# A two-layer graph kernel on one core: the last six adjacency blocks summed by column group, and what follows them reordered

## The chip, the cores and the metric

The kernel runs on one core of a Trainium2 chip. The metric is the device time of one execution in microseconds (us), smaller is better; times are medians of several runs. TensorE is called PE in the profile, VectorE DVE, ScalarE ACT, GpSimd POOL, SyncE SP. "PEld" is TensorE's weight load.

## The reference, cut to what matters

`x` is 4096 x 128, `adj` is 4096 x 4096, everything f32.

```python
def _gcn_norm_dense(adj):
    A = adj + jnp.eye(n)
    deg = A.sum(axis=1)
    d = jnp.where(deg > 0, jax.lax.rsqrt(deg), 0.0)
    return d[:, None] * A * d[None, :]
def _L0(x, adj, W1, b1, W2, b2):
    An = _gcn_norm_dense(adj)
    h = jax.nn.relu(An @ (x @ W1) + b1)
    return An @ (h @ W2) + b2                      # the second aggregation
def _L1(x, adj, ff0_w, ff1_w, attn_w, g1, b1, g2, b2):
    x_norm = _ln(x, g1, b1)
    mask = (adj > 0) | jnp.eye(n, dtype=bool)
    for i in range(K):                             # K = 2 heads
        h = x_norm @ ff0_w[i].T
        s_src, s_dst = h @ attn_w[i, :c], h @ attn_w[i, c:]
        e = leaky_relu(s_src[:, None] + s_dst[None, :])
        atten = softmax(where(mask, e, NEG), axis=1)
        att = _ln(atten @ h + x, g2, b2)
        h_next = h_next + jax.nn.elu(att @ ff1_w[i].T) / K
    return h_next
x = _layernorm(x + _L0(...)); x = _layernorm(x + _L1(x, adj, ...))
```

## The kernel before, in words

**Stages.** The 4096 nodes are 32 blocks of 128 rows, or 8 column groups of 512. The first aggregation reads all of `adj` and of its transpose and takes the degrees from them. The second reads the transpose again: each of 32 turns (a block of 128 x 4096, 2 MB) adds 8 matmuls of 128x512, one into each of PSUM's eight banks, so that bank k holds the sum of column group k. Each turn also makes the block's 0/1 mask in bytes and stores it in DRAM (`mask`, 0.5 MB). Then comes attention, whose passes of 4 phases x 16 chunks read the masks back: ScalarE makes `T` (two relus for a chunk), VectorE multiplies it by the mask, TensorE sums 4 matmuls of 128x512.

**What sets the order.** Every engine's program is written out by hand, with semaphores; an engine runs its list strictly in order, and a DMA is issued by the engine that stands in its place in the list (loads by SP, mask stores by ScalarE).

**The second aggregation.** Turns 0 to 3 use blocks still in `colbuf` (four slots), turns 4 and 5 the two slots of `rowbuf` (`AHEAD = 2`), turns 6 to 31 `colbuf` again. `reload` in the SP program (L321) loads the next block into a slot once TensorE (`pe_block`) and the mask of the slot's turn (`mask_made`) are done with it. VectorE adds the identity to the block's own columns (`add_self`, L747), on which TensorE waits (`own_ready`), and makes the mask (`make_mask`, L751 and L754) in one of two `mtile` slots, once the store of two turns ago has landed. ScalarE copies the turn's weights to `stat` and issues the store (`supply`, L497 and L499); its copy for a turn begins when TensorE has finished the turn before the last.

```python
AHEAD = LATE = 2
ROUNDS = NI - 2                 # NI = 8, four turns in a round
```

**The end of it.** The last `LATE = 2` turns go by column group (L1189): for group k, two matmuls, then for group k-1 the turn of the sum (`L1200`, four transposes), for group k-5 the turn of the normalised nodes (`L1206`), for group k-6 the source and target terms (`wag`, four matmuls of 128x4 into bank 0). Between them stand ScalarE's copies out of PSUM (L515, L519), VectorE's skip, statistics and normalisation (L795, L778, L785, L807) and GpSimd's inverse roots (L418 to L426, one group after the other). GpSimd's (POOL's) two powers for a group are `rstd` and `r2`.

**From there to the first chunk.** VectorE makes `st` from all terms (L815, L818) and its largest values over the free axis (`span`). TensorE turns `st`, ScalarE copies it to `s_rows` and stores it in DRAM (`s_src`), SP loads it back as `Rrow`, spread over all partitions (L337). GpSimd's `partition_all_reduce` (L428) gives the maximum over nodes, `top`. TensorE multiplies eight pairs of node blocks by `gff` into PSUM banks 4 to 7 (`multiply_z`, 0 to 7, 2 matmuls of 128x256 each), ScalarE copies them to `W` (`read_z`, L530); the other eight pairs follow one by one behind chunks 0 to 7, their copies behind relus 5 to 12. ScalarE then copies `mixed`, loads its table of exponentials, makes `ratio` and `weight` (L544, L545), the exponential of `Rrow` (L550) and the first relus (L558).

Of the kernel before, what the change touches and what calls it, by code (L numbers as in the profile page):

```python
# [16 lines left out]
F32 = mybir.dt.float32  # L17
# [3 lines left out]
ALU = mybir.AluOpType  # L21
# [3 lines left out]
P = 128  # L25
# [39 lines left out]
def build(nc, t, out):  # L65
# [16 lines left out]
    with ctx:  # L82
# [29 lines left out]
        half = sb("half", [P, B], F32)  # L112
        d_all = sb("d_all", [P, B], F32)
# [8 lines left out]
        span = sb("span", [P, 2 * K], F32)  # L122
        top = sb("top", [P, 2 * K], F32)
# [54 lines left out]
        Rrow = sb("Rrow", [P, 2, WIDE], F32)  # L178
# [8 lines left out]
        def sems(names):  # L187
# [19 lines left out]
            "x1_ready x1t_done x1T_ready st_done st_step st_ready s_turned s_copied s_stored")  # L207
        mix_turned, mixT_ready, mix_done, mix_ready, z_done, z_read = sems(
            "mix_turned mixT_ready mix_done mix_ready z_done z_read")
        span_step, span_ready, top_ready, npass_step, npass_ready = sems("span_step span_ready top_ready npass_step npass_ready")  # L210
# [49 lines left out]
        AHEAD = LATE = 2  # L260
        ROUNDS = NI - 2
# [4 lines left out]
        STATS, MOMENTS, SHIFT = 1, 2, 3  # L266
        TURN = SHIFT + 1
        ZR = B // 2
        Z_EARLY = 8
        PHASE = NC  # L270

        def more_passes(eng):

            eng.wait_ge(npass_ready, 1)
            return eng.value_load(npass[0:1, 0:1], min_val=0, max_val=MAX_PASSES)

# [21 lines left out]
        def _(sp):  # L298
# [45 lines left out]
            def phase(q, g, next_h, f):  # L344
                for c in range(NC):
# [4 lines left out]
                    if c == 6:  # L350
                        if not (isinstance(q, int) and g == 0):
                            sp.wait_ge(relu_made, at_turn(q * (G * NC) + g * NC))
                        source_row(next_h, (g + 1) % G)
                    if c == NC - 1 and f is not None:
                        store(f, (g - 2) % G)

            sp.wait_ge(agg_done, 2 * NG)
# [3 lines left out]
            sp.wait_ge(s_stored, 16)  # L361
            source_row(0, 0)
# [16 lines left out]
        def _(pool):  # L379
# [6 lines left out]
            pool.tensor_copy(ident_u8[:, :], ident[:, :]).then_inc(ident_ready, 1)  # L386
            pool.memset(keeps[:, 0:1], 1.0).then_inc(consts_ready, 1)
# [28 lines left out]
            for k in range(NG):  # L416
# [4 lines left out]
                pool.wait_ge(scale_ready, k + 1)  # L421
                r = r2[:, group(k)]
                pstep(pool.tensor_tensor(r, rstd[:, group(k)], rstd[:, group(k)], ALU.mult))
                pstep(pool.tensor_tensor(r, r, mv[:, group(k), 1], ALU.mult))  # L424
                pstep(pool.tensor_scalar(r, r, LN_EPS, 1.0, ALU.add, ALU.mult))  # L425
                pool.tensor_tensor(r, r, half[:, group(k)], ALU.pow).then_inc(r2_ready, 1)  # L426
            pool.wait_ge(span_ready, 1)
            pool.partition_all_reduce(top[:, :], span[:, :], P, bass.bass_isa.ReduceOp.max).then_inc(top_ready, 1)  # L428
# [34 lines left out]
        def _(act):  # L463
# [42 lines left out]
            for u in range(LATE):  # L506
                supply(B - LATE + u, u, ROUNDS * RING + AHEAD + u, u % SN)

            for i in range(NG + TURN + 2):
                k = i  # L510
                if k < NG:
                    act.wait_ge(agg_done, NG + k + 1)
                    if k >= SN:
                        act.wait_ge(tr_done, k - 1)
                    act.activation(hT[:, k % SN, :], ps[:, k, :], ACT.Copy).then_inc(accT_ready, 1)  # L515
                k = i - TURN - 1
                if 0 <= k < NG:
                    act.wait_ge(x1t_done, k + 1)
                    act.activation(x1T[:, cols(k, GW)], ps[:, k, :], ACT.Copy).then_inc(x1T_ready, 1)  # L519

            act.wait_ge(s_turned, 1)
            act.activation(s_rows[:, :], ps[0:K * B, 1, 0:P], ACT.Copy).then_inc(s_copied, 1)
            act.wait_ge(s_copied, 1)
            act.dma_start(s_dram.rearrange("k (b p) -> (k b) p", p=P), s_rows[:, :]).then_inc(s_stored, 16)
            act.wait_ge(mix_turned, 1)
            act.activation(mixT[:, :, :].rearrange("p k c -> p (k c)"), ps[:, 2, 0:K * C], ACT.Copy).then_inc(mixT_ready, 1)

            def read_z(r):
                act.wait_ge(z_done, r + 1)
                act.activation(W[:, Z0:Z1 + 1:2, 2 * r:2 * r + 2, :],  # L530
                               ps[:, 4 + r % 4, :].rearrange("p (b h c) -> p h b c", b=2, h=K), ACT.Copy).then_inc(z_read, 1)

            for r in range(Z_EARLY):
                read_z(r)
            act.wait_ge(mix_done, 1)
            for head in range(K):
                at = head * C
                act.activation(mixed[:, head, at:at + C], ps[:, 3, cols(head)], ACT.Copy).then_inc(mix_ready, 1)
# [115 lines left out]
        def _(v):  # L654
# [114 lines left out]
            for u in range(LATE):  # L769
                v.wait_ge(col_loaded[u], 16 * (NI + 1 + ROUNDS))  # L770
                add_self(colbuf[:, u, :], ROUNDS * RING + AHEAD + u)
                v.wait_ge(own_ready, ROUNDS * RING + AHEAD + u + 1)
                make_mask(B - LATE + u, colbuf[:, u, :], ROUNDS * RING + AHEAD + u, u % SN, 16 * ((B - LATE + u) // SN + 1))
# [16 lines left out]
            for i in range(NG + 3):  # L790
                k = i
                if k < NG:
                    v.wait_ge(tr_done, k + 1)
                    for b in range(k * BPG, (k + 1) * BPG):
                        last = v.scalar_tensor_tensor(out=x1[:, b, :], in0=ps[:, k, cols(b % BPG)],  # L795
                                                      scalar=d_all[:, b:b + 1], in1=x1[:, b, :],
                                                      op0=ALU.mult, op1=ALU.add)
                    last.then_inc(rows_ready, 1)
                if 0 <= i - STATS < NG:
                    stats(i - STATS)  # L800
                if 0 <= i - MOMENTS < NG:
                    moments(i - MOMENTS)
                if 0 <= i - SHIFT < NG:
                    k = i - SHIFT
                    v.wait_ge(scale_ready, k + 1)
                    for b in range(k * BPG, (k + 1) * BPG):
                        last = v.tensor_scalar(x1[:, b, :], x1[:, b, :], mv[:, b, 0:1], rstd[:, b:b + 1],  # L807
                                               ALU.subtract, ALU.mult)
                    last.then_inc(x1_ready, 1)


            v.wait_ge(st_done, NG)
            v.wait_ge(r2_ready, NG)
            v.wait_ge(consts_ready, 5)
# [198 lines left out]
            v.wait_ge(top_ready, 1)  # L1013
            v.tensor_copy(gref[:, CUR:CUR + 1], top[:, 0:1]).then_inc(gref_step, 1)
            v.tensor_copy(gref[:, TOP1:TOP1 + 1], top[:, 1:2])
            v.wait_ge(gref_step, 1)
            set_window(0, 0)
            set_inside(0, 0, 0)
            set_inside(0, 0, 1)
            cap_row(0, 0)  # L1020
# [296 lines left out]
```

## Time and profile before

| | us |
|---|---|
| median of 3 runs (lowest, highest) | 1063.94 (1062.9, 1065.08) |
| the profiled execution, its own time | 1063.9 |
| its span, first to last instruction | 1062.1 |
| TensorE busy in the span | 986.0 (93%) |
| VectorE, ScalarE, GpSimd busy | 701.0, 499.0, 113.6 |
| mean granted clock of TensorE | 0.967 of full |

Times in the rows count from the span's start. The second aggregation runs from 288.4 to some 500 us, the first chunk begins at 554.59 us. In a timeline row, "x8" merges eight records in a row, the number in square brackets is the engine's idle time before the first and what ended it. One f32 matmul of the program leaves two records, each transpose one. In a row of windows, "PEclk" is the granted clock as a share of full speed.

### The profile page before, as it was taken

What the parts mean: (1) busy time and instruction counts of PE and PEld (TensorE: products, weight loads), DVE (VectorE), ACT (ScalarE), POOL (GpSimd) and SP (SyncE); (2) the same over time, 40 slices, a digit from 0 to 9 for tenths busy, and PEclk for the clock granted to TensorE, in tenths of its full rate; (3) what the DMA queues carried; (4) which work ended last, traced back from release to release, by engine and by line L of the source; (5) the groups of instructions that cost most, each with busy time, mean ns of one, the idle gap of its engine ahead of it and who ended that gap; (6) DMA issues with size and microseconds to landing.
All of it is one profiled execution on the core that took longest, in us unless ns stands there. A gap on an engine that the chain in (4) does not pass through costs nothing.

```text
span 1062.1 us, 9255 instructions
## 1 busy us (share of the span) xinstructions
PE 986.0 (93%) x2590; PEld 477.6 (45%) x2592; DVE 701.0 (66%) x1251; ACT 499.0 (47%) x723; POOL 113.6 (11%) x144
## 2 busy tenths in 40 slices
PE   5789999999999999999769999999999999999980
PEld 4334444444644444444655444444545444444440
DVE  0567766654355444344737767888799998988874
ACT  3433332221200000001266765978686888888754
POOL 0011111111040000000800000000010101010111
PEclk8899999999999999999769999999999999999995
DMA  9999999999286999995023131222222232323201
GB/s 347 427 426 427 428 426 425 425 422 388 110 322 256 371 377 383 385 380 213 1 70 99 62 97 59 91 79 97 72 70 86 84 99 89 99 90 100 84 5 40
DMA packets 62202, 226.03 MB, mean 213 GB/s; under 512 B 4496, under 2 KB 44112, under 8 KB 52048
## 3 DMA queue, kind: packets, MB, share of 16 engines
q1 hardware_dynamic: 57040, 208.56, 51.3%
q10 hardware_dynamic: 5120, 17.01, 4.0%
q8 instruction: 15, 0.25, 0.1%
q14 instruction: 27, 0.22, 0.1%
HBM read 205.59 MB, written 19.96 MB: 212 GB/s over the span
## 4 chain that ended last, share of the span: by engine, by line
PE 77%; DMA 11%; ACT 5%; POOL 3%; issue 2%; DVE 2%; SPq 1%; POOLq 0%; ACTq 0%; DVEq 0%
PE ps L1096 77%; DMA W<-in_adj 11%; ACT W L478 2%; POOL rstd L419 1%; POOL r L426 1%; ACT T L558 1%; ACT final L604 1%; SPq L302 0%; DVE T L870 0%; ACT mix L587 0%; ACT squares L578 0%; POOL rs L437 0%; POOL r L424 0%; POOL r L425 0%; POOLq L82 0%
## 5 line engine op out<-in xcount | busy, mean ns | idle before, releaser
L1096 PE MATMUL ps<-colbuf,stat 128*128 128x512 f32 x992 | 441.9, 602 | 25.3 <-DVE diag L712 24.8
L1096 PE MATMUL ps<-T,Yw 128*128 128x512 f32 x1024 | 445.1, 594 | 9.2 <-DVE T L870 9.2
L870 DVE SCALAR_TENSOR_TENSOR T<-T,mring 128x2048 f32<-128x2048 f32 x128 | 292.5, 2287 | 66.6 <-ACT T L558 65.9
L558 ACT ACTIVATE T<-Rrow,small,ratio 128x1024 f32<-128x1024 f32 x256 | 301.3, 1230 | 70.7 <-PE ps L1096 70.4
L1096 PEld LDWEIGHTS ps<-T,Yw 128*128 128x128 f32 x1024 | 195.4, 191 | 245.4 <-issue 230.7
L1096 PEld LDWEIGHTS ps<-colbuf,stat 128*128 128x128 f32 x992 | 187.9, 193 | 248.9 <-issue 220.8
L478 ACT ACTIVATE W<-W 128x4096 f32<-128x4096 f32 (+30 forms) x32 | 66.1, 2067 | 147.7 <-DMA W<-in_adj 147.7
L497 ACT ACTIVATE stat<-xw_g 128x128 f32 (+1 forms) x32 | 9.9, 310 | 197.8 <-PE ps L1096 167.8
L751 DVE TENSOR_SCALAR mtile<-colbuf 128x4096 uint8<-128x4096 f32 x30 | 69.7, 2323 | 11.6 <-DMA mask<-mtile 9.7
L747 DVE TENSOR_TENSOR colbuf<-colbuf,ident 128x128 f32 (+1 forms) x26 | 7.6, 291 | 88.3 <-DMA colbuf<-in_adjT 88.3
L672 DVE TENSOR_TENSOR W<-W,colbuf 128x3712 f32<-128x3712 f32 (+28 forms) x29 | 62.3, 2148 | 0.0
L394 POOL PARTITION_ALL_REDUCE colrow<-W x30 | 32.2, 1073 | 217.1 <-DVE W L672 186.3
L434 POOL TENSOR_SCALAR rs<-sumsq 128x4 f32<-128x4 f32 x16 | 14.3, 892 | 346.6 <-ACT squares L578 225.9
L683 DVE TENSOR_SCALAR small<-rowpart,colpart 128x1 f32<-128x1 f32 x30 | 6.4, 214 | 60.5 <-ACT W L478 60.4
L1096 PE MATMUL ps<-mixed,numS 128*128 (+1 forms) x128 | 30.6, 382 | 3.1 <-DVE A L933 1.9
L1096 PEld LDWEIGHTS ps<-mixed,numS 128*128 128x128 f32 x128 | 24.2, 190 | 13.6 <-issue 8.5
L945 DVE SCALAR_TENSOR_TENSOR mix<-A,inv,W 128x256 f32<-128x256 f32 x64 | 26.7, 480 | 3.3 <-DVE inv L940 3.1
L587 ACT ACTIVATE mix<-mix,rs 128x128 f32<-128x128 f32 (+1 forms) x64 | 20.4, 390 | 14.9 <-POOL rs L437 14.5
L604 ACT ACTIVATE final<-W,fin_shift,fin_scale 128x128 f32 (+1 forms) x48 | 19.5, 480 | 16.3 <-DVE fin_shift L992 16.0
L418 POOL TENSOR_SCALAR rstd<-mv 128x4 f32<-128x4 f32 x8 | 1.5, 194 | 196.7 <-DVE mv L785 196.1
L710 DVE TENSOR_TENSOR colbuf<-colbuf,ident 128x128 f32<-128x128 f32 x32 | 9.3, 292 | 16.7 <-DMA colbuf<-in_adjT 15.9
L860 DVE TENSOR_SCALAR Yw<-W,r2w,weight 128x128 f32<-128x128 f32 x64 | 19.0, 338 | 0.2
(150 smaller groups left out, 581.5 us busy)
## 6 DMA issues: line engine op xcount, KB each, us to landing
colbuf<-in_adjT SPq DMA_DIRECT2D x58, 2048.0 KB, 13.2
mring<-mask SPq DMA_DIRECT2D x128, 256.0 KB, 2.7
mask<-mtile ACTq DMA_DIRECT2D x32, 512.0 KB, 10.2
Rrow<-s_src SPq DMA_DIRECT2D x9, 512.0 KB, 4.1
W<-in_adj SPq DMA_DIRECT2D x2, 2048.0 KB, 14.7
W<-in_adjT SPq DMA_DIRECT2D x2, 2048.0 KB, 12.7
out<-final SPq DMA_DIRECT2D x6, 512.0 KB, 3.9
W<-in_xT SPq DMA_DIRECT2D x8, 256.0 KB, 6.9
```

Source lines behind the costliest of these rows:

```text
L394: pool.partition_all_reduce(colrow[:, b % 2, :], colacc[:, cols(b)], P, bass.bass_isa.ReduceOp.add)\
L434: pool.tensor_scalar(rs[:, half_of(part)], sumsq[:, half_of(part)], 1.0 / C, LN_EPS, ALU.mult, ALU.add)\
L478: act.activation(row, row, ACT.Copy, accum_out=rowpart[:, b % 2:b % 2 + 1]).then_inc(rowsum_done, 1)
L558: last = act.activation(T[:, c % TS, j, :], Rrow[:, g % 2, :], ACT.Relu, scale=ratio[:, c * JB + j:c * JB + j + 1], bias=small[:, 8:9])
L587: last = act.activation(mix[:, i, bass.ds(1 - h, 1), :].rearrange("p o c -> p (o c)"), mix[:, i, bass.ds(h, 1), :].rearrange("p o c -> p ( ...
L604: last = act.activation(final[:, i, :], W[:, bass.ds(dst, 1), k * GB + i, :].rearrange("p o c -> p (o c)"), ACT.Identity, scale=fin_scale[ ...
L672: v.tensor_tensor(colacc[:, lo:], colacc[:, lo:], colbuf[:, u, lo:], ALU.add).then_inc(colacc_done, 1)
L751: v.tensor_scalar(mtile[:, tile, :], block, 0.0, None, ALU.is_gt).then_inc(tile_step, 1)
L860: last = v.tensor_scalar(Yw[:, b, :], x1[:, b, :], r2w[:, b:b + 1], weight[:, b:b + 1], ALU.mult, ALU.add)
L870: v.scalar_tensor_tensor(out=tile, in0=tile, scalar=1.0, in1=mring[:, c % TS, :, :].rearrange("p b n -> p (b n)"), op0=ALU.add, op1=ALU.mu ...
L945: last = v.scalar_tensor_tensor(out=mix[:, i, :, :], in0=A[:, b, 0:2 * C].rearrange("p (o c) -> p o c", o=2), scalar=inv[:, i:i + 1], in1= ...
L1096: return pe.matmul(*args, skip_group_check=True, **kw)
```

## The change

Names are those of the changed kernel.

- `ROUNDS` is one less and `LATE` is 6: turns 26 to 31 are done by column group. Two of their blocks (26, 27) are loaded into `rowbuf` early, behind turns 4 and 5, the other four (22 to 25) into `colbuf` behind turns 22 to 25. Groups 0 and 1 take their first five matmuls each before either takes its sixth. The weights come straight from `xw_g`.
- VectorE adds the identity to all six blocks first, then makes the six masks.
- ScalarE issues the six stores, runs one small Exp (which loads its table), and only then copies sum 0.
- Skip, statistics and normalisation of a group follow each other on VectorE; the last two groups are interleaved; GpSimd puts off `r2` of the last two groups.
- Source terms of nodes 0 to 1023 are made, turned, stored and loaded ahead (`early_*`).
- The maximum over nodes: `span` turned by TensorE, a `tensor_reduce` on 4 partitions, and a matmul of `ones` by a diagonal of 4 columns.
- Z products 0 to 12 stand before chunk 0, between the turns of the last groups; three of them (10 to 12) are copied by VectorE; 13 to 15 follow chunks 0 to 2, their copies stand behind relus 1 to 3.

```diff
-        AHEAD = LATE = 2
-        ROUNDS = NI - 2
+        AHEAD = 2
+        LATE = AHEAD + RING
+        ROUNDS = NI - 3
-        Z_EARLY = 8
+        Z_FIRST, Z_MOVED, Z_BANKS = 10, 3, 4
+        Z_WAITING = Z_FIRST + Z_MOVED
+        EARLY = 6
 # SP, behind the first four reloads
+            for n in range(AHEAD):
+                sp.wait_ge(pe_block, RING + n + (1 + MASK_CREDIT))
+                sp.wait_ge(mask_made, RING + n + (1 + MASK_CREDIT))
+                sp.dma_start(late(n)[0], dram_block(adj_cols, late(n)[1])).then_inc(row_loaded[n], 16)
 # POOL
-            pool.partition_all_reduce(top[:, :], span[:, :], P, bass.bass_isa.ReduceOp.max).then_inc(top_ready, 1)
 # ACT
-            for u in range(LATE):
-                supply(B - LATE + u, u, ROUNDS * RING + AHEAD + u, u % SN)
+            for n in range(LATE):
+                turn = B - LATE + n
+                act.wait_ge(mask_made, turn + (1 + MASK_CREDIT))
+                act.dma_start(dram_block(mask_dram, late(n)[1]), mtile[:, turn % SN, :]).then_inc(mask_stored[turn % SN], 16)
+            act.wait_ge(zeros_ready, 2)
+            act.activation(small[:, 11:12], small[:, 8:9], ACT.Exp)
...
-                    if g == 0 and 5 <= c < 5 + ZR - Z_EARLY:
-                        read_z(Z_EARLY + c - 5)
+                    if g == 0 and 1 <= c <= ZR - Z_WAITING:
+                        read_z(Z_WAITING + c - 1)
 # DVE
+            for n in range(LATE):
+                block, b = late(n)
+                if n < AHEAD:
+                    v.wait_ge(row_loaded[n], NI * 32 + 32)
+                else:
+                    v.wait_ge(col_loaded[n - AHEAD], 16 * (NI + 1 + ROUNDS))
+                add_self(block, b)
+            for n in range(LATE):
+                turn = B - LATE + n
+                block, b = late(n)
+                v.wait_ge(own_ready, turn - RING + 1)
+                make_mask(turn, block, b, turn % SN, 16 * (turn // SN + 1))
...
+            v.wait_ge(span_turned, 1)
+            v.tensor_reduce(highest[:, :], ps[0:2 * K, 6, 0:P], AX_X, ALU.max).then_inc(top_step, 1)
...
+            for r in range(Z_FIRST, Z_FIRST + Z_MOVED):
+                v.wait_ge(z_done, r + 1)
+                v.tensor_copy(W[:, Z0:Z1 + 1:2, 2 * r:2 * r + 2, :],
+                              ps[:, 2 + r % Z_BANKS, :].rearrange("p (b h c) -> p h b c", b=2, h=K)).then_inc(z_moved, 1)
 # PE
+            for k in range(2):
+                late_sums(k, range(LATE - 1))
+            for k in range(2):
+                late_sums(k, [LATE - 1])
+            turn_sums(0)
+            for k in range(2, NG):
+                late_sums(k, range(LATE // 2))
+                turn_sums(k - 1)
+                late_sums(k, range(LATE // 2, LATE))
+                turn_nodes(k - 2)
+                if k == EARLY - 1:
+                    pe.wait_ge(early_ready, 1)
+                if k >= 3:
+                    sources(k - 3)
+                if k == EARLY:
+                    pe.transpose(ps[0:GB, 1, 0:P], early_st[:, :], ident[:, :]).then_inc(early_turned, 1)
+            turn_sums(NG - 1)
...
+            turn_nodes(NG - 2)
+            multiply_z(2)
+            sources(NG - 2)
+            for r in range(3, 7):
+                multiply_z(r)
+            turn_nodes(NG - 1)
+            multiply_z(7)
+            sources(NG - 1)
+            multiply_z(8)
...
-                    if g == 0 and c < ZR - Z_EARLY:
-                        multiply_z(Z_EARLY + c)
+                    if g == 0 and c < ZR - Z_WAITING:
+                        multiply_z(Z_WAITING + c)
```

ScalarE at the end of the second aggregation; `hT` is the copy of a group's sum, `W` here the copy of its turned nodes. Before:

```order
111 L497 ACTIVATE stat<-xw_g 128x128
112 L499 DMA mask<-mtile 128x4096
113 L497 ACTIVATE stat<-xw_g 128x128
114 L499 DMA mask<-mtile 128x4096
115 L515 ACTIVATE hT<-ps 128x512 x6
```

And in the changed kernel:

```order
111 L539 DMA mask<-mtile 128x4096 x6
112 L541 ACT_TABLE_LOAD
113 L541 ACTIVATE small<-small 128x1
114 L547 ACTIVATE hT<-ps 128x512 x3
115 L551 ACTIVATE W<-ps 128x512
```

Six stores and the table load, where two stores were, now stand ahead of the first copy of a sum.

VectorE in the same place of the changed kernel, with its waits; before, each addition of the identity (L747) was followed by its own block's mask (L751, L754):

```order
512 L793 TENSOR_TENSOR colbuf<-colbuf,ident 128x128 [waits col_loaded2]
513 L793 TENSOR_TENSOR colbuf<-colbuf,ident 128x128 [waits col_loaded3]
514 L797 TENSOR_SCALAR mtile<-W 128x4096 [waits mask_stored0,own_ready]
515 L800 TENSOR_TENSOR mtile<-mtile,ident_u 128x128 [waits tile_step]
516 L797 TENSOR_SCALAR mtile<-W 128x4096 [waits mask_stored1,own_ready]
517 L800 TENSOR_TENSOR mtile<-mtile,ident_u 128x128 [waits tile_step]
```

Even the masks of the two blocks that were loaded early (`W`) now stand behind the wait for the last block to arrive (`col_loaded3`).

ScalarE at the first chunks (`T` a relu, `W` the copy of a z product). Before:

```order
130 L558 ACTIVATE T<-Rrow,small,ratio 128x1024 x12
131 L530 ACTIVATE W<-ps 128x2x256
132 L558 ACTIVATE T<-Rrow,small,ratio 128x1024 x2
```

And in the changed kernel:

```order
140 L604 ACTIVATE T<-Rrow,small,ratio 128x1024 x4
141 L555 ACTIVATE W<-ps 128x2x256
142 L604 ACTIVATE T<-Rrow,small,ratio 128x1024 x2
143 L555 ACTIVATE W<-ps 128x2x256
```

The first copy of a z product stood behind the relus of six chunks; it now stands behind those of two.

## Rows read from the trace of the kernel before

**Rows 1.** The page's busy times, then the chain of waits, in order of time

```profile
PE 986.0 (93%) x2590; PEld 477.6 (45%) x2592; DVE 701.0 (66%) x1251; ACT 499.0 (47%) x723; POOL 113.6 (11%) x144
...
286.68 207.69 PE ps L1096 x487
...
554.59 94.61 PE ps L1096 x240
```

**Rows 2.** Timeline of ScalarE from 465 us: the copy that begins when turn 25 ends

```profile
467.02 0.31 ACT L497 ACTIVATE stat<-xw_g 128x128 f32 x1 [6.56 <-PE ps L1096]
```

**Rows 3.** VectorE's timeline: identity additions in turns 29 and 31, each ending a load's wait

```profile
477.92 0.29 DVE L747 TENSOR_TENSOR colbuf<-colbuf,ident 128x128 f32 x1 [3.53 <-DMA colbuf<-in_adjT]
...
491.14 0.29 DVE L747 TENSOR_TENSOR colbuf<-colbuf,ident 128x128 f32<-128x128 f32 x1 [3.98 <-DMA colbuf<-in_adjT]
```

**Rows 4.** Instructions on `colbuf`, 286 to 500 us: time of its loads

```profile
DMA to landing us min/median/max: 8.5/10.7/11.4
```

**Rows 5.** VectorE's timeline: the second and third mask, whose stores meet no loads

```profile
292.62 2.29 DVE L751 TENSOR_SCALAR mtile<-colbuf 128x4096 uint8<-128x4096 f32 x1
...
295.44 2.29 DVE L751 TENSOR_SCALAR mtile<-colbuf 128x4096 uint8<-128x4096 f32 x1 [0.21 <-DMA mask<-mtile]
```

**Rows 6.** Windows: span of time, PE, PEld, DVE, ACT, POOL busy, clock, DMA share, GB/s

```profile
326.00:330.00 4.00, 4.00 (x11) 1.85 (x10) 3.23 (x4) 0.00 (x0) 0.00 (x0) 1.00 0.05 18
...
516.00:520.00 4.00, 2.44 (x23) 2.21 (x22) 4.00 (x21) 1.10 (x2) 3.42 (x8) 1.00 0.00 0
...
524.00:536.00 12.00, 9.86 (x47) 9.61 (x47) 3.50 (x16) 1.79 (x3) 7.42 (x16) 0.50 0.01 1
...
548.00:552.00 4.00, 0.00 (x0) 0.00 (x0) 0.99 (x4) 3.86 (x6) 0.00 (x0) 0.87 0.00 0
```

**Rows 7.** Timeline of the last two turns, by group (PE), with ScalarE's copy

```profile
496.83 0.60 ACT L515 ACTIVATE hT<-ps 128x512 f32<-128x512 f32 x1 [2.14 <-PE ps L1096]
...
498.35 0.60 PE L1200 MATMUL ps<-ident,hT 128*128 128x128 f32 x4
...
498.79 1.88 PE L1096 MATMUL ps<-colbuf,stat 128*128 128x512 f32 x4
...
500.51 0.60 PE L1200 MATMUL ps<-ident,hT 128*128 128x128 f32 x4
...
512.28 0.95 PE L1096 MATMUL ps<-wag,W 128*128 128x4 f32 x8
```

**Rows 8.** Timeline from the last source terms to the maximum over nodes

```profile
536.21 0.29 DVE L815 TENSOR_TENSOR st<-ps,r 128x128 f32<-128x128 f32 x1 [4.42 <-PE ps L1096]
...
538.60 0.39 POOL L428 PARTITION_ALL_REDUCE top<-span  x1 [5.95 <-issue]
```

**Rows 9.** Timeline from the last z copy before the chunks to chunk 1

```profile
544.00 0.75 DVE L844 TENSOR_SCALAR Rrow<-Rrow,gref 128x1024 f32<-128x1024 f32 x1 [4.06 <-DMA Rrow<-s_src]
...
546.48 0.44 ACT L538 ACTIVATE mixed<-ps 128x128 f32<-128x128 f32 x2
546.94 1.28 ACT L544 ACT_TABLE_LOAD   x1
548.24 0.23 ACT L544 ACTIVATE ratio<-below 128x32 f32<-128x32 f32 x1
...
548.62 1.06 ACT L550 ACTIVATE Rrow<-Rrow 128x1024 f32<-128x1024 f32 x1
...
552.25 2.29 DVE L870 SCALAR_TENSOR_TENSOR T<-T,mring 128x2048 f32<-128x2048 f32 x1 [2.57 <-ACT T L558]
...
554.59 5.26 PE L1096 MATMUL ps<-T,Yw 128*128 128x512 f32 x8 [8.20 <-DVE T L870]
```

**Rows 10.** Timeline of TensorE, then of ScalarE, at the first chunks

```profile
559.69 1.03 PE L1096 MATMUL ps<-gff,W 128*128 128x256 f32 x4
560.55 3.60 PE L1096 MATMUL ps<-T,Yw 128*128 128x512 f32 x8
...
564.19 2.38 ACT L558 ACTIVATE T<-Rrow,small,ratio 128x1024 f32<-128x1024 f32 x2 [1.93 <-PE ps L1096]
```

More of the change, by code:

```diff
@@ L332, in _ @@
                     reload(u, i * RING + (AHEAD + u), i * RING + (AHEAD + u))
-            for u in range(LATE):
+            for u in range(RING):
                 reload(u, ROUNDS * RING + AHEAD + u, ROUNDS * RING + AHEAD + u)
@@ L350, in phase @@
                     if c == 6:
-                        if not (isinstance(q, int) and g == 0):
+                        if isinstance(q, int) and g == 0:
+                            sp.wait_ge(s_stored, 16)
+                        else:
                             sp.wait_ge(relu_made, at_turn(q * (G * NC) + g * NC))
@@ L414, in pstep, with scale_rows @@
                 pool.wait_ge(pool_step, done[0])
-            for k in range(NG):
+            def scale_rows(k):
                 pool.wait_ge(moments_ready, k + 1)
@@ L789, in _, with add_skip @@
             v.wait_ge(skip_ready, NG)
[L790 to L809, printed above, removed]
+            def add_skip(k):
+                v.wait_ge(tr_done, k + 1)
+                for b in range(k * BPG, (k + 1) * BPG):
+                    last = v.scalar_tensor_tensor(out=x1[:, b, :], in0=ps[:, k, cols(b % BPG)],
+                                                  scalar=d_all[:, b:b + 1], in1=x1[:, b, :],
+                                                  op0=ALU.mult, op1=ALU.add)
+                last.then_inc(rows_ready, 1)
+                stats(k)
+                moments(k)
@@ new lines, in late_sums @@
+            def late_sums(k, some):
+                for n in some:
+                    block, b = late(n)
+                    if k == 0:
+                        if n < AHEAD:
+                            pe.wait_ge(row_loaded[n], NI * 32 + 32)
+                        else:
+                            pe.wait_ge(col_loaded[n - AHEAD], 16 * (NI + 1 + ROUNDS))
+                        pe.wait_ge(own_ready, ROUNDS * RING + AHEAD + n + 1)
+                    last = multiply(ps[:, k, :], xw_g[:, b, :], block[:, cols(k, GW)], start=False, stop=n == LATE - 1)
+                if n == LATE - 1:
+                    last.then_inc(agg_done, 1)
@@ new lines, in turn_sums, with turn_nodes @@
+            def turn_sums(k):
+                pe.wait_ge(accT_ready, k + 1)
+                for ib in range(BPG):
+                    last = pe.transpose(ps[:, k, cols(ib)], hT[:, k % SN, cols(ib)], ident[:, :])
+                last.then_inc(tr_done, 1)
+            def turn_nodes(k):
+                pe.wait_ge(x1_ready, k + 1)
+                for ib in range(BPG):
+                    last = pe.transpose(ps[:, k, cols(ib)], x1[:, k * BPG + ib, :], ident[:, :])
+                last.then_inc(x1t_done, 1)
@@ new lines, in sources, with multiply_z @@
+            def sources(k):
+                pe.wait_ge(x1T_ready, k + 1)
+                for ib in range(BPG):
+                    b = k * BPG + ib
+                    last = multiply(ps[:, 0, cols(b, 2 * K)], x1T[:, cols(b)], wag[:, :], start=True, stop=True)
+                last.then_inc(st_done, 1)
+            def multiply_z(r):
+                if r >= Z_FIRST + Z_BANKS:
+                    pe.wait_ge(z_moved, r - Z_FIRST - Z_BANKS + 1)
+                elif r >= Z_BANKS:
+                    pe.wait_ge(z_read, r - Z_BANKS + 1)
+                for i in range(2):
+                    last = multiply(ps[:, 2 + r % Z_BANKS, cols(i, 2 * C)], x1T[:, cols(2 * r + i)],
+                                    gff[:, :, :].rearrange("p k c -> p (k c)"), start=True, stop=True)
+                last.then_inc(z_done, 1)
@@ L1225, in multiply_z @@
[L1225 to L1234 removed]
+            multiply_z(0)
+            multiply_z(1)
@@ L1240, in chunk @@
+            multiply(ps[:, 7, 0:2 * K], ones[0:2 * K, :], top_diag[:, :], start=True, stop=True).then_inc(top_done, 1)
+            for r in range(11, Z_WAITING):
+                multiply_z(r)
+            pe.wait_ge(s_copied, 1)
+            pe.wait_ge(mix_ready, K)
             def chunk(q, g, c):
```

202 lines of the change are left out of this document (110 added, 92 removed).

## The prediction

> **What bounds the kernel now.** I read the page's busy times first, then the chain of waits: TensorE is busy for 93% of the span, and nearly the whole second aggregation is one piece of the chain on TensorE, 207.69 us long [rows 1]. The reader should see that no other engine matters there as long as it stays ahead; that holds until 494.4 us. The chain is TensorE's again from the first chunk at 554.59 us on. So the change is worth what it does between the end of turn 25, where the two programs part, and the first chunks, and I lay out that stretch step by step from timelines. Everything behind it only shifts.
>
> **Start: 467.0 us.** ScalarE's copy at 467.02 began when turn 25 ended [rows 2]. SP's last but two reload began at the same moment; in the changed kernel it is the last one, and brings the sixth block.
>
> **Edits that I cost at nothing.** The two early loads (4 MB) are issued at about 323 and 330 us, where the DMA engines fall idle (share 0.05 in 326 to 330) [rows 6]. What they delay is covered by slack: turn 29's identity addition stood at 477.92 [rows 3], and its matmuls began at 467.0 + 3 x 6.87 = 487.6, so loads were 9.7 us early. Were the cover gone (all 4 MB, some 10 us by the load times [rows 4], fall on one turn), it would cost under 1 us. Weights straight from `xw_g` save ScalarE small copies that were off the path.
>
> **1. The sixth block.** TensorE does ten matmuls of 0.86 (two in 498.79 to 500.51 [rows 7]) until 475.6. The load issued at 467.0 was in before at 477.9, 10.9 later [rows 3]; beside it ran a following load and three mask stores that are gone. The quickest load took 8.5 [rows 4]. Between 475.5 and 477.9 I take 476.5; with the diagonal (0.3) 476.8. TensorE takes the two last matmuls and **stops at 478.6** in front of the turn of sum 0.
>
> **2. Six masks.** VectorE's order puts all masks behind the sixth diagonal. The second mask began at 292.62 and the third at 295.44, with only 0.21 of wait for a store [rows 5]: 2.82 each where stores meet no loads, as here. 6 x 2.82 = 16.9, so the last ends at about 493.6. In the kernel before all but the last of them lay beside TensorE's turns. Below, the mask instruction alone gives 2.29 x 6 (3 us less); above, stores of some 4.5 instead of 2.7 us give 2.5 us more.
>
> **3. ScalarE in front of sum 0.** It issues the sixth store (0.35), loads the table (1.28 [rows 9]), runs the small Exp (0.25), and copies the sum (0.60 [rows 7]): 496.1. TensorE has then **waited 17.5 us**. Queued behind that wait are all its remaining sums, and behind them VectorE and GpSimd.
> The table load stood between 546.92 (end of the copy of `mixed`) and 548.24: 1.30 in all [rows 9]. The Trainium skill (ScalarE: Activation LUTs, What ACT_TABLE_LOAD costs) adds a drain to the load, 2.66 us together. This trace does not agree; by the page the sum would be 1.4 us more.
>
> **4. The clock.** With TensorE idle in 548 to 552 the granted clock fell (0.87 of the window) to its lower level, 1.2 GHz, and chunk 0 took 554.59 to 559.69, 5.1 us for four matmuls that take 3.43 at the upper level [rows 6, 9, 10]. A wait of 17.5 us will do the same: 1.7 us on the late sums and 0.4 on the first transposes; 2.0, between 1.5 and 4.
>
> **5. Groups 2 to 7.** 36 matmuls x 0.86 = 30.9; seven turned sums and six turned nodes x 0.44 (498.35 to 498.79 [rows 7]) = 5.7; five source terms x 0.81 (eight records, 0.95 with their tail [rows 7]) = 4.1; the early transpose 0.1. Together 40.8, plus 2.0: **538.9**. VectorE needs some 2.5 us, GpSimd 1.3 and VectorE 1.1 per group, against 6.8 of TensorE, so nobody waits here. That is the gain of the change: GpSimd's 3.4 us per group, which in 516 to 536 held TensorE at 61 to 82% busy [rows 6], lie under matmuls.
>
> **6. To the last source terms.** Three turns (1.3), three source terms (2.4), the `mixed` work (0.6), z 0 to 7 (8 x 0.86 = 6.9 [rows 10]): 11.2, and 1.0 for ScalarE's copies that stand in the way: 551.1.
>
> **7. To the maximum.** Before, `st` began at 536.21 and the maximum was in use at 539.0 by GpSimd's reduction [rows 8]. Now z 8, a turn, z 9 and a second turn (2.1) stand in TensorE's list, then four small steps with their hand-overs (1.4): 554.6, 3.5 us after the terms. It took 2.8 before; the reduction by TensorE gains nothing here.
>
> **8. To chunk 0.** `below` (0.3) and the row's cap (0.75): 555.7, the early row being there, where the row was waited for 4.06 us before [rows 9], beside the z copies. Exponential 1.1, two relus 2.4: 559.2. VectorE's three z copies end at about 559.5 (0.6 to 0.7 each, ScalarE's 128x512 copy being nearest [rows 7]; at twice that, 1.5 us more). Mask 2.29: **chunk 0 at 561.7**, against 554.6 [rows 9]: **+7.1**.
>
> **9. Behind it.** Three z products instead of eight: -5 x 0.86 = **-4.3**. But ScalarE's copy of z 13 stands behind relu 1, and z 13 behind chunk 0. Chunk 0 ends at 565.1, z 13 at 566.0, its copy 566.9, relu 2 569.3, mask 2 571.5, while TensorE, with chunk 1 and z 14 done at 570.3, waits 1.2 us. The copy of z 15 holds relu 4 in the same way: z 15 ends at 575.9, relu 4 at 579.1, mask 4 at 581.4, chunk 3 at 579.3: 2.1 us. Before, four chunks' relus ran ahead and twelve stood in front of the first copy; ScalarE's wait of 1.93 was for a free tile [rows 10]. **+3.3**.
>
> **10. The clock at chunk 0.** It cost 1.7 us before, after 8.20 us of idle time [rows 9]; now TensorE is idle for 5.0, which may or may not suffice. -1.7 to 0: **-0.8**.
>
> **Sum:** 7.1 - 4.3 + 3.3 - 0.8 = +5.3 us. Against the profiled execution's own time, 1063.9 (the median is 1063.94): **1069.2 us**. With the bounds of steps 1, 2, 4 and 10 the case reaches from 1066.1 to 1073.
>
> **The rivals.**
> - *Faster: TensorE is not held at sum 0.* The wait of 17.5 us is the price of the order of masks and stores; without it the change gains. Had only the sixth mask to follow the last block, the copy would come at about 482 and no clock would be lost: 14 + 2 less, 1053. The change breaks even where the sixth mask ends by 488.3 instead of 493.6, and is faster by over 0.2% from 486.2 on. Against it: VectorE's and ScalarE's lists are in order, and no row has a mask below 2.29. For it: VectorE idles over 3 us in every turn [rows 3], so the time is there if some wait is not what I take it for. 0.12, with small errors to that side.
> - *Slower still: the clock falls in the tail.* In 516 to 520 TensorE was busy for 61% with transposes and source terms, and in 524 to 536 the clock was 0.50 though it was 82% busy [rows 6]. From 538.9 on such work is mixed with z products. At the lower level until some 550, steps 6 and 7 take 5.5 us more: 1074.7. The Trainium skill (TensorE: Matmul & The Clock Gate, Part 4) says that transposes don't count as activity for the clock, by which this case would be likelier; the z products in between speak against it. 0.13.
> - *No change that can be measured.* Masks, load and clock at their kind ends give 3.1 less, 1066.1; a further 1 us from step 8 or 9 leaves a difference within 0.2% (2.1 us, about what a measurement of this kernel can tell from no change). This is also the case in which the new waits only take the place of the old. 0.13.
> - My forecast: 0.62.
>
> **How the numbers follow.** Slower by over 0.2%: 0.62 + 0.13 = 0.75; within: 0.13; faster: 0.12. The range runs from 1061.5, which takes in the case of no change and the nearest part of the faster one, to 1075.0, which takes in the fallen clock.
>
> **What would show it.** In the changed kernel's timeline: a wait of TensorE of 15 to 20 us at the first turned sum, ended by ScalarE's `hT`; six masks some 2.8 us apart behind the last identity addition at about 477; a lower clock behind it; then TensorE over 95% busy from 500 to 538; chunk 0 at about 562; waits of TensorE for VectorE's masks at chunks 2 and 4, and of ScalarE for TensorE ahead of the z copies. The forecast is wrong if the first turned sum comes before 488, if chunk 0 comes before 557, or if TensorE stalls in turns 6 to 25.

## The result, and the profile after

| | kernel before | changed kernel |
|---|---|---|
| median, us (lowest, highest) | 1064.71 (1062.9, 1065.46), 5 runs | 1069.20 (1069.03, 1070.92), 5 runs |
| ratio of the times, 95% interval | | 1.0045 [1.0034, 1.0056] |
| span of the profiled execution, us | 1062.1 | 1067.3 |
| TensorE busy in the span, us | 986.0 | 982.9 |
| mean granted clock | 0.967 | 0.968 |

The change makes the kernel slower by 0.45%, which is 4.8 us [3.6, 6.0]. TensorE has 3 us less to do than in [rows 1] and yet the program ends later: the time went into waits.

**The waits at the first turned sum.** These are rows of the timelines of VectorE, TensorE and ScalarE in the changed kernel (start, duration, what ran, and in brackets the idle time before it and what ended it); they answer to [rows 3, 5, 7].

```profile
477.05 0.29 DVE L793 TENSOR_TENSOR colbuf<-colbuf,ident 128x128 f32<-128x128 f32 x1 [6.81 <-DMA colbuf<-in_adjT]
477.26 2.29 DVE L797 TENSOR_SCALAR mtile<-W 128x4096 uint8<-128x4096 f32 x1
477.49 1.95 PE L1170 MATMUL ps<-colbuf,xw_g 128*128 128x512 f32 x4 [1.54 <-DVE colbuf L793]
...
482.68 2.29 DVE L797 TENSOR_SCALAR mtile<-colbuf 128x4096 uint8<-128x4096 f32 x1 [0.28 <-DMA mask<-mtile]
...
488.09 2.29 DVE L797 TENSOR_SCALAR mtile<-colbuf 128x4096 uint8<-128x4096 f32 x1 [0.26 <-DMA mask<-mtile]
493.64 1.28 ACT L541 ACT_TABLE_LOAD   x1 [39.56 <-DVE mtile L800]
495.68 1.12 PE L1275 MATMUL ps<-ident,hT 128*128 128x128 f32 x4 [16.23 <-ACT hT L547]
```

The last identity addition is at 477.05. Behind it stand six masks, two every 5.4 us, then the table load, the small Exp and the copy of sum 0. TensorE has nothing to do for 16.23 us, though every sum of groups 0 and 1 was complete at 479.4.

**What the change gains, and what the clock does.** Windows of the changed kernel (span of time; busy PE, PEld, DVE, ACT, POOL; granted clock; DMA share; GB/s), answering to [rows 6]:

```profile
326.00:330.00 4.00, 4.00 (x11) 1.83 (x10) 0.89 (x1) 0.00 (x0) 0.00 (x0) 1.00 1.01 371
484.00:488.00 4.00, 0.00 (x0) 0.00 (x0) 3.77 (x4) 0.00 (x0) 0.00 (x0) 0.50 0.46 186
504.00:538.00 34.00, 34.00 (x137) 19.17 (x136) 18.07 (x86) 5.81 (x12) 14.69 (x31) 1.00 0.05 16
538.00:558.00 20.00, 18.19 (x109) 15.37 (x107) 9.41 (x41) 11.46 (x22) 4.52 (x8) 1.00 0.17 55
562.00:566.00 4.00, 4.00 (x6) 1.85 (x7) 3.17 (x6) 0.00 (x0) 0.00 (x0) 0.63 0.26 71
```

The early loads fill the hole at 326 us, and TensorE stays busy there throughout. During the long wait the granted clock falls to 0.50, the lower level of 1.2 GHz. The restart shows what that costs: the first turned sum and the three matmuls behind it take 5.25 us (495.68 to 500.93), 2.2 more than at the upper level. Then comes the gain: from 504 to 538 TensorE is busy all the time at the upper level. Before, it was busy for 61% in 516 to 520, and in 524 to 536 for 82% at a clock of 0.50 [rows 6].

**From the last source terms to the chunks.** Timeline rows of the changed kernel, answering to [rows 8 to 10]:

```profile
551.34 0.29 DVE L879 TENSOR_TENSOR st<-ps,r 128x128 f32<-128x128 f32 x1 [6.74 <-PE ps L1170]
554.56 0.16 DVE L1082 COPY gref<-ps 128x1 f32<-128x1 f32 x1 [0.64 <-PE ps L1170]
557.24 1.88 DVE L1094 COPY W<-ps 128x512 f32<-128x512 f32 x3
562.00 5.16 PE L1170 MATMUL ps<-T,Yw 128*128 128x512 f32 x8 [5.54 <-DVE T L934]
568.05 0.60 ACT L555 ACTIVATE W<-ps 128x512 f32<-128x512 f32 x1 [6.46 <-PE ps L1170]
573.36 3.70 PE L1170 MATMUL ps<-T,Yw 128*128 128x512 f32 x8 [1.04 <-DVE T L934]
577.96 0.60 ACT L555 ACTIVATE W<-ps 128x512 f32<-128x512 f32 x1 [2.75 <-PE ps L1170]
```

Chunk 0 begins at 562.00, 7.4 us later than before [rows 9]. ScalarE, next in line with the copy of z 13, stands idle for 6.46 us; the mask of chunk 2 is late for it, and behind the copy of z 15 (577.96) that of chunk 4 too. The chain of waits of the changed kernel (start, duration, what) shows the same, and then one piece without a break:

```profile
562.00 6.04 PE ps L1170 x12
...
573.36 4.58 PE ps L1170 x12
...
583.26 450.37 PE ps L1170 x1104
```

### The profile page after: what moved, and what is told of

It reads as the page before. It is cut to its first block, busy times and chain, and to the rows that moved or that the text cites. A ratio compares the mean times of both kernels' runs of the same rounds, so it can differ in the third digit from the quotient of the medians.

```text
span 1067.3 us, 9202 instructions
## 1 busy us (share of the span) xinstructions
PE 982.9 (92%) x2596; PEld 470.8 (44%) x2596; DVE 705.5 (66%) x1259; ACT 495.5 (46%) x716; POOL 113.2 (11%) x140
## 4 chain that ended last, share of the span: by engine, by line
PE 76%; DMA 15%; ACT 5%; DVE 3%; issue 1%; SPq 0%; POOL 0%; POOLq 0%; ACTq 0%; DVEq 0%
PE ps L1170 75%; DMA W<-in_adj 13%; ACT W L508 3%; DMA colbuf<-in_adjT 1%; DVE mtile L797 1%; DVE T L934 1%; ACT T L604 1%; ACT final L650 1%; DMA mask<-mtile 1%; SPq L317 0%; PE ps L1275 0%; PE ps L1281 0%; ACT mix L633 0%; ACT squares L624 0%; POOL rs L467 0%
## 5 line engine op out<-in xcount | busy, mean ns | idle before, releaser
L1170 PE MATMUL ps<-colbuf,stat 128*128 128x512 f32 x896 | 399.9, 603 | 24.7 <-DVE diag L758 24.6
L1170 PEld LDWEIGHTS ps<-colbuf,stat 128*128 128x128 f32 x896 | 169.9, 193 | 228.9 <-issue 200.8
L797 DVE TENSOR_SCALAR mtile<-colbuf 128x4096 uint8<-128x4096 f32 x28 | 65.2, 2329 | 18.6 <-DMA mask<-mtile 17.2
L1170 PE MATMUL ps<-colbuf,xw_g 128*128 128x512 f32 x64 | 30.1, 595 | 1.5 <-DVE colbuf L793 1.5
L547 ACT ACTIVATE hT<-ps 128x512 f32<-128x512 f32 x8 | 4.6, 594 | 35.8 <-PE ps L1170 35.8
```

Of the source, the lines that this page charges most:

```text
L797: v.tensor_scalar(mtile[:, tile, :], block, 0.0, None, ALU.is_gt).then_inc(tile_step, 1)
L1170: return pe.matmul(*args, skip_group_check=True, **kw)
```

## The experiments

Each kernel is the changed one with the edit that is shown, unless it says otherwise. "Ratio" is against the kernel before, with its 95% interval; the changed kernel itself has 1.0045 [1.0034, 1.0056]. The edits are shortened. The masks' order is the suspect for the largest term, so it comes first.

### Masks between the identity additions

```diff
-for n in range(LATE): late_self(n)
-for n in range(LATE): late_mask(n)
+S0 S1 M0 M1 S2 S3 M2 S4 M3 S5 M4 M5      # S: identity, M: mask, on VectorE
```

> The changed kernel with four of the six late masks made while the loads are awaited; masks 4 and 5 stay behind the last identity addition. Theory A (TensorE's wait of 16.23 us at the first turned sum is the price of six masks of 2.7 us in front of ScalarE's copy): the wait falls to 5 to 6 us, the sixth mask ends at about 482.6 instead of 493.2, the time falls by 10.6 us, and by up to 2 more if the clock stays up: 1057.5 us (1056 to 1059.5). Theory B (the order by column group holds TensorE anyway, by the chain copy, skip, GpSimd, normalise of each group; the mask wait only hides it): the wait reappears in groups 2 to 7, and the time falls by under 4 us: 1065 or more.

Measured: 1064.19 us (1062.15 to 1068.47, 10 runs), ratio 0.9993 [0.9981, 1.0004]. Some 5 us better than the changed kernel; less than half of the gain that was expected. Its timeline (VectorE, TensorE) tells why:

```profile
471.54 2.29 DVE L797 TENSOR_SCALAR mtile<-colbuf 128x4096 uint8<-128x4096 f32 x1 [4.20 <-DMA mask<-mtile]
...
474.50 2.05 PE L1174 MATMUL ps<-colbuf,xw_g 128*128 128x512 f32 x2 [3.89 <-DVE colbuf L793]
477.41 2.29 DVE L797 TENSOR_SCALAR mtile<-colbuf 128x4096 uint8<-128x4096 f32 x1 [3.05 <-DMA mask<-mtile]
484.77 2.29 DVE L797 TENSOR_SCALAR mtile<-colbuf 128x4096 uint8<-128x4096 f32 x1 [2.01 <-DMA mask<-mtile]
...
489.83 1.11 PE L1279 MATMUL ps<-ident,hT 128*128 128x128 f32 x4 [5.65 <-ACT hT L547]
```

There are two mask tiles. A mask has to wait until the store of two masks ago has landed, and beside the blocks' loads such a store took up to 10.4 us here, against 2.7 where it met none. That wait is now in front of the identity additions, and TensorE waits for those (3.89). So the order can't be judged without the number of tiles: with two of them there is a choice between late masks and late diagonals.

### Six mask tiles

```diff
-mtile = sb("mtile", [P, 2, N], U8, first)
+mtile = sb("mtile", [P, 6, N], U8, first)
+S0 S1 M0 M1 S2 S3 M2 S4 M3 M4 S5 M5      # only M5 behind the last identity addition
```

> The changed kernel with six mtile slots and five of the six late masks in front of the last identity addition; stores as before, each behind its mask, ahead of the copy of sum 0. In the first try at this a mask waited 3 to 4 us for the landing of a store that shared the DMA engines with the loads, and the diagonals behind it waited too. Theory A2 (with two tiles, masks beside loads are paced by their stores; with six they are not): no wait for a store, TensorE's wait at the first turned sum under 5 us, though the stores delay the last load by some 3 us: copy of sum 0 at some 485.4 instead of 495.1, 10 us less, up to 2 more for the clock: 1058.5 us (1056.5 to 1060). Theory B (the mask work is bound by the DMA engines themselves, so tiles don't matter): as the first try, 1063 to 1065.

Measured: 1056.26 us (1054.79 to 1058.79, 4 runs), ratio 0.9927 [0.9908, 0.9947]: 12.9 us less than the changed kernel, and faster than the kernel before. TensorE and ScalarE in its timeline:

```profile
478.27 1.96 PE L1177 MATMUL ps<-colbuf,xw_g 128*128 128x512 f32 x4 [1.49 <-DVE colbuf L795]
...
481.18 1.28 ACT L543 ACT_TABLE_LOAD   x1 [27.16 <-DVE mtile L803]
483.21 0.66 PE L1282 MATMUL ps<-ident,hT 128*128 128x128 f32 x4 [2.99 <-ACT hT L549]
```

The last block is as late as in the changed kernel, but the turned sum comes at 483.21, 12.5 us sooner. This shows that the masks' place and their tiles were the cause, and not the load. The two weren't changed one by one: against the kernel with two tiles, mask 4 has moved too, and no run has six tiles with all masks last. There the tiles could save little, since in the changed kernel the late masks waited for stores only 0.28 and 0.26 us.

### ScalarE's first copies ahead of the stores

```diff
+copy_sum(0); copy_sum(1)
 for n in range(LATE): late_store(n)
 act.activation(small[:, 11:12], small[:, 8:9], ACT.Exp)
```

> The changed kernel with ScalarE's copies of sums 0 and 1 ahead of its six mask stores; VectorE's order unchanged. Theory A, by VectorE: TensorE gets its first turned sum at about 480.5 and does group 2, then waits for the turned nodes of group 0, since VectorE's skip stands behind the six masks; it resumes near 498.5 with group 3, about 5.5 us ahead of the changed kernel: 1064 us (1062.5 to 1065.5). Rival, ScalarE alone holds it: about 15 us less, 1054.

Measured: 1065.25 us (1063.48 to 1067.37, 10 runs), ratio 1.0004 [0.9995, 1.0013]. The first turned sum began at 477.38, at once behind the sums, but the wait only moved one step on: VectorE's work on the group stands behind its masks. TensorE's timeline:

```profile
495.93 1.11 PE L1289 MATMUL ps<-ident,W 128*128 128x128 f32 x4 [12.32 <-DVE W L864]
```

Some 4 us are regained by the medians: work of the next groups fits in before the wait. In this execution the last block had also landed 2.3 us sooner (its identity addition is at 474.74).

### Copies of the last z products later

```diff
-if g == 0 and 1 <= c <= ZR - Z_WAITING: read_z(Z_WAITING + c - 1)
+if g == 0 and 5 <= c < 5 + ZR - Z_WAITING: read_z(Z_WAITING + c - 5)
```

> The changed kernel with the copies of z 13 to 15 behind relus 5 to 7 instead of 1 to 3. Theory A: TensorE's waits for masks 2 and 4 (1.0 us and some 2 us) go, relus 2 and 3 run ahead: 3.3 us less, 1065.9 us (1065 to 1067). Rival: TensorE is held there by VectorE's masks whatever ScalarE does, or the copies cost the same later: 1068.5 to 1069.5.

Measured: 1064.72 us (1062.97 to 1066.33, 11 runs), ratio 0.9998 [0.9989, 1.0007], so 4.5 us better than the changed kernel where 3.3 were expected. In its chain both gaps are gone:

```profile
560.62 469.67 PE ps L1170 x1148
```

TensorE's timeline shows what the time of one execution also holds:

```profile
560.62 6.69 PE L1170 MATMUL ps<-T,Yw 128*128 128x512 f32 x8 [5.54 <-DVE T L934]
567.15 1.03 PE L1170 MATMUL ps<-gff,W 128*128 128x256 f32 x4
```

Chunk 0 began 1.38 us sooner than in the changed kernel, mostly because the last block landed 1.0 us sooner, but it took 6.53 us up to z 13 against 4.99, after the same 5.54 us of idle time. The later matmuls come 3.3 us sooner (`mixed` by `numS` at 647.01, against 650.33). So the gaps are worth 3.3 - 1.4 + 1.5, some 3.5 us; the rest of the 4.5 is not explained.

### The maximum by GpSimd again

```diff
+pool.partition_all_reduce(top[:, :], span[:, :], P, bass.bass_isa.ReduceOp.max)
-pe.transpose(ps[0:2 * K, 6, 0:P], span[:, :], ident[:, :])
-v.tensor_reduce(highest[:, :], ps[0:2 * K, 6, 0:P], AX_X, ALU.max)
-multiply(ps[:, 7, 0:2 * K], ones[0:2 * K, :], top_diag[:, :], start=True, stop=True)
```

> The changed kernel with the maximum over nodes by GpSimd's partition_all_reduce, as before, instead of by TensorE. Theory A (TensorE's way gains nothing): from the end of span at 552.5 us GpSimd needs 1.6 us to the first use, TensorE's way takes 2.0: within 0.5 us of 1069.2, rather below. Rival (TensorE's way was worth having): 1.5 us or more above, 1070.7.

Measured: 1069.38 us (1068.73 to 1071.22, 5 runs), ratio 1.0039 [1.0025, 1.0053]: no difference from the changed kernel. But it isn't that nothing changed. In its timeline the maximum is in use 1.3 us sooner than at 554.56; later, a row of GpSimd is strange:

```profile
552.84 0.39 POOL L460 PARTITION_ALL_REDUCE top<-span  x1 [6.58 <-DVE span L889]
...
573.30 3.70 PE L1167 MATMUL ps<-T,Yw 128*128 128x512 f32 x8 [1.04 <-DVE T L936]
...
667.09 0.19 POOL L466 TENSOR_SCALAR rs<-sumsq 128x4 f32<-128x4 f32 x1 [113.86 <-issue]
```

Chunk 0 began at 561.16, 0.8 us sooner than in the changed kernel, but took 5.78 us up to z 13 (566.94, against 566.99), where it was 4.99. So in this execution the gain was used up by the clock, and chunk 2 is where it was (573.30 against 573.36). And GpSimd's first row scale of the attention waits for nothing that the profile shows ("issue"); it is taken up below.

### The row of sources not early

```diff
-source_row(0, 0)                                      # ahead of the masks' waits
+sp.wait_ge(s_stored, 16); source_row(0, 0)            # behind the whole store
```

> The changed kernel with the first Rrow loaded only once all source terms are stored, as before (the early store still runs). Theory A: the load is then issued some 2 us behind ScalarE's store at 554.06 us and takes some 4 more, so the cap comes at 560.8 instead of 554.97, and chunk 0 at 567.6 instead of 562.0: 5.6 us more, 1074.8 us (1073.5 to 1076.5); the early terms are worth that. Rival: the row was not what chunk 0 waited for, under 1 us more.

Measured: 1073.74 us (1072.54 to 1073.91, 4 runs), ratio 1.0086 [1.0069, 1.0102], 4.5 us above the changed kernel. VectorE's timeline shows the wait of [rows 9] back, somewhat longer:

```profile
558.43 0.75 DVE L909 TENSOR_SCALAR Rrow<-Rrow,gref 128x1024 f32<-128x1024 f32 x1 [5.03 <-DMA Rrow<-s_src]
```

Chunk 0 began at 565.45, 3.4 us later than in the changed kernel, and took 1.0 us longer up to z 13 (6.02 against 4.99). So the early source terms are worth some 3.4 to 4.5 us here, less than the 5.6 expected; the prediction named the wait of 4.06 that they take away.

### All three repairs

Six tiles with their order, small Exp and copies 0 and 1 ahead of the stores, and the z copies later:

> The six tiles and the masks' order of the run above, ScalarE's small Exp ahead of everything else there, its copies of sums 0 and 1 ahead of all six stores, and the copies of z 13 to 15 behind relus 5 to 7. Theory A: TensorE's wait at the first turned sum under 1.5 us (15 less), no fall of the clock there (1.6 less), no waits at chunks 2 and 4 (4.5 less): 1048 us (1046 to 1051), faster than both kernels. Theory B (groups 2 to 7 are then held by the chain of each group, or the gains hide one another): 1054 or more.

Measured: **1047.24 us** (1046.43 to 1047.65, 4 runs), ratio 0.9838 [0.9821, 0.9854], 17.2 us under the kernel before. A window and a row of TensorE's timeline:

```profile
484.00:488.00 4.00, 4.00 (x17) 2.24 (x16) 2.52 (x14) 1.08 (x2) 2.28 (x4) 1.00 0.82 322
```

```profile
478.33 0.65 PE L1290 MATMUL ps<-ident,hT 128*128 128x128 f32 x4
```

The turned sum has no wait in front of it, and in 484 to 488 TensorE is busy throughout, at a clock of 1.00 where the changed kernel had 0.50.

### With GpSimd's maximum

The same with GpSimd's reduction as above:

> The kernel of the run above with GpSimd's maximum over nodes. In the changed kernel GpSimd's way brought the maximum 1.3 us earlier and chunk 0 0.8 us earlier, but the clock ate it. Expected 0.8 us less than the run above, 1047.2 us, within 0 to 2.0 less; that TensorE's way is the better one would show as more.

Measured: 1047.09 us (1046.84 to 1047.86, 4 runs), ratio 0.9838 [0.9821, 0.9854]: the same. GpSimd's and TensorE's timelines have the strange row again, and what follows from it:

```profile
643.80 0.19 POOL L468 TENSOR_SCALAR rs<-sumsq 128x4 f32<-128x4 f32 x1 [109.14 <-issue]
...
651.25 20.87 PE L1182 MATMUL ps<-T,Yw 128*128 128x512 f32 x48 [1.23 <-DVE T L951]
```

### One small step of GpSimd behind its reduction

In all kernels with that delay the last thing GpSimd had done was the `partition_all_reduce`; in the others it was a tensor instruction. The first kernel is the one just above, the second is the kernel before, each with this line:

```diff
 pool.partition_all_reduce(top[:, :], span[:, :], P, bass.bass_isa.ReduceOp.max)
+pstep(pool.tensor_scalar(rs[:, 0:BPG], half[:, 0:BPG], 1.0, 1.0, ALU.mult, ALU.mult))
```

> The three changes together and GpSimd's reduction, plus one small tensor_scalar of GpSimd (128x4, its result unused) right behind the partition_all_reduce. Theory: GpSimd's first ordinary tensor instruction behind a partition_all_reduce starts late, once, wherever it stands; the small step takes that delay at 535 us, under the z products and relus, so the first rs follows ScalarE's squares within 0.5 us (it was held for 7.08 us in the chain of waits without it), TensorE's stall behind it is gone, and the time is about 0.9 us below the kernel without the step: about 1046.2. Rival: the delay belongs to the first row scale itself (first of its kind, after 100 us without work); then it stays, with 1047.1.

> The kernel before with the same small step behind its own partition_all_reduce. Theory of the switch: the small step itself starts late (some 6 us after the reduction, at about 545 us), the row scale at 653 us follows the squares at once, the 0.98 us stall of TensorE at 667.34 is gone, and the time is about 1.0 us below the kernel before: about 1063.5, ratio 0.999. Rival: no difference, stall still there.

Measured: **1045.06 us** (1044.14 to 1046.55, 5 runs), ratio 0.9818 [0.9805, 0.9832], the fastest of this study; and 1063.43 us (1062.46 to 1064.69, 11 runs), ratio 0.9987 [0.9978, 0.9996], for the kernel before with the line alone. GpSimd's timeline in the first:

```profile
538.60 1.02 POOL L463 TENSOR_SCALAR rs<-half 128x4 f32<-128x4 f32 x1 [6.72 <-issue]
634.13 1.10 POOL L469 TENSOR_SCALAR rs<-sumsq 128x4 f32<-128x4 f32 x1 [94.51 <-ACT squares L637]
```

and in the second:

```profile
548.67 0.19 POOL L429 TENSOR_SCALAR rs<-half 128x4 f32<-128x4 f32 x1 [9.05 <-issue]
653.75 1.10 POOL L435 TENSOR_SCALAR rs<-sumsq 128x4 f32<-128x4 f32 x1 [104.88 <-ACT squares L579]
```

The delay has moved to the small step, where nobody waits, and the row scale follows ScalarE's squares. In both chains TensorE's piece from chunk 0 on has no break; that of the second reads

```profile
555.32 472.54 PE ps L1097 x1168
```

The first kernel gained 2.0 us where 0.9 were expected. In its profiled execution the copy of sum 0 came 2.8 us sooner than in that of the kernel above it, because its last blocks landed sooner; loads differ by such amounts between executions, and the two intervals overlap. What is shown is the stall that is gone, not the whole 2.0.

## Why the prediction was right, step by step

The forecast was slower by 5.3 us; measured are 4.8 [3.6, 6.0], and the spans of the profiled executions differ by 5.2. Its cause, the six masks behind the last diagonal, is the one that the experiments confirm: with another place for them and enough tiles the same change is faster than the kernel before. That the total came so near is in part luck: terms of up to 1.3 us were wrong and nearly cancel. Of the single steps:

- *Steps 1 to 3.* The last masks ended at 493.2 (493.6 forecast), the turned sum came at 495.68 (496.1), the wait was 16.23 us (17.5). Two small errors cancel here: the sixth block was ready some 0.5 us later, and the six masks took 16.0 us rather than 16.9, since only every second of them waited for a store. The table load took 1.28 us and the Exp began 0.01 us behind it, so the drain of the Trainium skill (ScalarE: Activation LUTs, What ACT_TABLE_LOAD costs) isn't seen here either.
- *Steps 4 and 5.* Sum 7 was turned at 538.93 (538.9 forecast). From the first turned sum that is 43.2 us, against 40.8 of work; of the 2.4 us more the clock cost 2.2 at the restart, where 2.0 were forecast.
- *Steps 6 to 8.* `st` at 551.34 (551.1), the maximum at 554.56 (554.6), chunk 0 at 562.00 (561.7).
- *Step 9.* TensorE's idle times at chunks 2 and 4 are 1.04 and 1.91 us. Counted from starts, with 0.86 us for a z product and 3.43 for a chunk, the delays are 1.22 and 2.07, 3.3 together, as forecast.
- *Step 10 was mis-sized.* Chunk 0 took 4.99 us up to z 13, against 5.10 before. The term is -0.1 and not -0.8 in this pair of executions. It isn't a fixed price: after the same 5.54 us of idle time chunk 0 took between 4.99 and 6.53 us in the six traces that have it.
- *A term was missing.* By these steps the sum is 7.4 - 4.3 + 3.3 - 0.1 = 6.3, and the matmuls of `mixed` by `numS` that follow come 6.46 us later (650.33 against 643.87). The kernel before, however, then loses a microsecond that the changed one doesn't: the next such matmuls come only 5.21 us later (693.26 against 688.05), which is the whole difference of the spans. Rows of its chain of waits and of TensorE's timeline:

```profile
653.05 6.62 issue
659.68 0.42 POOL rs L434
...
667.34 13.14 PE L1096 MATMUL ps<-T,Yw 128*128 128x512 f32 x30 [0.98 <-DVE T L870]
```

  In the changed kernel GpSimd's row scale follows the squares, and TensorE has no stall:

```profile
659.44 1.08 POOL L464 TENSOR_SCALAR rs<-sumsq 128x4 f32<-128x4 f32 x1 [113.35 <-ACT squares L624]
```

  So step 7 missed something where it said that the reduction by TensorE gains nothing: it is 1.3 us slower at the maximum, and it spares the program this stall 110 us later. That stall is shown by the traces and by the two kernels with the small step; in the times of the kernel with GpSimd's maximum, 1 us can't be told from its interval. The missing term (-1.25, of which the row shows 0.98 as idle time) and the mis-sized ones (+0.7 in step 10, +0.3 up to chunk 0) nearly cancel, and so the total came out right with these errors in it. The 0.3 us of the missing term that are no idle time have no cause in the rows.

*The range of the case.* Its bounds don't follow from those of the steps. Added up, the kind ends of steps 1, 2, 4 and 10 give 1.0 + 3.0 + 0.5 + 0.9 = 5.4 us less (1063.8), and the other ends 1.4 + 2.5 + 2.0 + 0.8 = 6.7 more (1075.9), not 1066.1 and 1073.

**The rivals.** The faster one named its own condition, the masks not holding TensorE, with 1053. That condition had to be made (six tiles: 1056.3), and it was the clue to the repair; that VectorE's idle time suffices for the masks was true, but not with two tiles. The rival of the fallen clock fell: in 538 to 558 the clock was 1.00. The Trainium skill (TensorE: Matmul & The Clock Gate, Part 4) says that transposes don't count as activity; this stretch can't decide on that, since z products stand between the transposes.

## What to carry to other kernels

Long work that is put behind short work pays only if it isn't itself the next thing that somebody waits for, and put in between it needs enough tiles never to wait for a store. When a large rearrangement gives nothing, look for the longest new wait: of the 22 us between the changed kernel and the repaired one (1047.24), 12.9 came with the shortening of the wait of 16.23 us. Where a stretch changed by more than the total, compare the later phases of both traces too; the other half of the sum can be a stall 100 us away.

## What was not expected of the hardware

- **GpSimd's first tensor instruction behind a reduction comes 6.6 to 9.1 us late, whenever it is asked for.** It came 6.72 and 9.05 us after the reduction in the kernels with the small step, and 6.6 to 7.6 us late in the chains of waits where it was the row scale, some 100 us later: idle time doesn't hide it. One cheap instruction right behind the reduction does, and was worth 1.4 us [0.4, 2.3] in the kernel before. The traces name what stands there: a MODIFY_POOL_CONFIG of GpSimd's queue, in front of the first instruction after each change between the two kinds. In the kernel before, at the reduction (L428), at the row scale (L434), and once more where nobody waits for it, behind the reductions at 288 us:

```profile
L428 POOLq MODIFY_POOL_CONFIG  x2: 7/7/7, 532.9 to 532.9; - x2
...
L434 POOLq MODIFY_POOL_CONFIG  x2: 11/11/11, 653.0 to 653.0; - x2
...
297.09 12.42 POOL L405 TENSOR_TENSOR W<-W,b2bc 128x512 f32<-128x512 f32 x8 [6.92 <-issue]
```

  The one at L434 comes at 653.0, just behind the squares, and not behind the reduction that ended at 539.0; the row scale follows it by 6.6 us. In the changed kernel there is none after 290.6. On the way there it came at 532.9, while `span` was still being made, so it is partly or wholly hidden: the reduction began 5.95 us after the last power, with `span` ready 1.2 us earlier [rows 8], and in the kernel with GpSimd's maximum, where `span` came later, 0.14 us behind it. The Trainium skill (GPSIMD Engine Reference, 2.1 Instruction dispatch) gives 5.95 us from MODIFY_POOL_CONFIG to the first call of a freshly loaded kernel. By these rows it is 5.7 us (532.9 to 538.60) on the way there, and 6.6 and more on the way back, which isn't on that page; and it isn't paid once: 32 reductions had run before the one at 538.60.
- **A store of 0.5 MB landed in 2.7 us alone and in up to 10.4 us beside loads.** Instructions on `mask`, 455 to 500 us, in the kernel with the masks between the additions:

```profile
DMA to landing us min/median/max: 2.7/4.5/10.4
```

- **What the lower clock costs at a restart varies between executions.** Chunk 0 takes 3.43 us at the upper level. After 5.54 us without work on TensorE it took 4.99, 5.31, 5.94, 6.11, 6.45 and 6.53 us in six traces, so 1.6 to 3.1 more; after 8.20 us, 5.10 and 5.16. Part of the spread of the times may be this, and one profiled execution can't price such a term to better than some 1.5 us.
